# A hybrid two-layer model on one core: outer products of the palette stage taken over four parts of the array, and all engines' pieces in another order

## The reference, cut to what matters

```python
topk_val, topk_idx = jax.lax.top_k(logits, K)            # K = 15 nearest earlier tokens of every token
G = clip(einsum('bhtkd,bhtjd->bhtkj', P_sel_norm, P_sel_norm), -1, 1)
rel = concatenate([G, feat_a, delta]); h = gelu(rel @ W1 + b1); h = gelu(h @ W2 + b2)
z = tanh(h @ Wc + bc);  w = softmax(h @ Wm + bm)         # a point (gx, gy) and a weight for each neighbour
samples = bilinear samples of palette (128 x 16 x 16) at the 15 points
V = einsum('btkd,btk->btd', samples, w);  y = V @ Wo
```

## Time and profile before

| what | us |
|---|---|
| median of 3 runs | 1595.28 (1595.07 to 1597.09) |
| the profiled execution's own time | 1594.69 |
| its span, first to last instruction | 1592.5 |
| PE busy / DVE busy / ACT busy / POOL busy | 1301.1 / 1089.6 / 842.2 / 902.2 |
| mean granted TensorE clock, share of 2.4 GHz | 0.873 |

### The profile page before, as it was taken

The page is one execution under the profiler, slowest core; times in us unless marked ns, Lnnn a source line. Parts: engine busy times, 40 slices in busy tenths (PEclk is TensorE's granted clock), DMA queues, the critical chain, the costliest instruction groups (busy, mean ns, idle before and its releaser), DMA issues.

```text
span 1592.5 us, 47322 instructions
## 1 busy us (share of the span) xinstructions
PE 1301.1 (82%) x18392; PEld 861.7 (54%) x18501; DVE 1089.6 (68%) x4635; ACT 842.2 (53%) x2247; POOL 902.2 (57%) x1398
## 2 busy tenths in 40 slices
PE   3667678797889788887979798898978988788886
PEld 1333445454556555656556464656546565656654
DVE  2788677687778778787777777877866755464452
ACT  1233344464475555657564655475654646456665
POOL 2445666576658566666646565656645446455431
PEclk9686778897989889898989898898968888899999
DMA  5000000100000000000000000000000000000000
GB/s 159 2 1 10 27 18 18 29 9 23 6 25 9 25 7 17 17 11 24 17 22 8 18 14 14 20 7 24 9 18 14 7 27 10 26 15 21 5 3 7
DMA packets 27211, 29.57 MB, mean 19 GB/s; under 512 B 12097, under 2 KB 22114, under 8 KB 26978
## 3 DMA queue, kind: packets, MB, share of 16 engines
q0 software_dynamic: 8304, 16.73, 3.8%
q1 hardware_dynamic: 18674, 9.72, 2.2%
HBM read 25.11 MB, written 2.29 MB: 17 GB/s over the span
## 4 chain that ended last, share of the span: by engine, by line
PE 47%; DVE 22%; issue 10%; ACT 8%; POOL 8%; another core or an unknown queue 1%; SPq 1%; DMA 1%; DVEq 0%; POOLq 0%; ACTq 0%
DVE ps L963 4%; PE ps L665 3%; PE ps L523 3%; PE ps L717 3%; PE ps L747 3%; PE ps L563 3%; DVE ps L955 3%; PE ps L739 2%; PE ps L690 2%; PE ps L577 2%; PE ps L587 2%; PE ps L604 2%; PE ps L855 2%; ACT sb L1602 1%
## 5 line engine op out<-in xcount | busy, mean ns | idle before, releaser
L963 DVE TENSOR_TENSOR_SCAN ps<-ps,sb 128x47 f32<-128x47 f32 (+3 forms) x1024 | 271.3, 265 | 43.6 <-DVE ps L955 0.5
L1792 POOL DMA_INDIRECT sb<-table,sb x240 | 240.8, 1003 | 98.9 <-issue 55.3
L955 DVE TENSOR_TENSOR ps<-sb,ps 128x24 f32<-128x24 f32 (+3 forms) x1024 | 193.7, 189 | 15.4
L1656 POOL TENSOR_TENSOR sb<-sb 128x1 f32<-128x1 f32 x128 | 73.1, 571 | 221.4 <-DVE sb L898 220.7
L523 PE MATMUL ps<-sb 128*128 128x512 bf16 x496 | 162.0, 438 | 16.6 <-issue 10.2
L587 PEld LDWEIGHTS ps<-sb 32*32 32x32 f32 x2032 | 43.3, 110 | 123.9 <-issue 66.1
L577 PE MATMUL ps<-sb 32*32 32x32 f32 x2032 | 71.5, 213 | 41.5 <-DVE sb L935 34.6
L577 PEld LDWEIGHTS ps<-sb 32*32 32x32 f32 x2032 | 42.5, 111 | 113.2 <-DVE sb L935 58.5
L587 PE MATMUL ps<-sb 32*32 32x12 f32 x2032 | 65.5, 190 | 46.0 <-DVE sb L971 34.6
L1301 ACT ACTIVATE sb<-sb 128x128 f32<-128x128 f32 x128 | 62.9, 493 | 73.1 <-POOL sb L1658 72.8
L523 PEld LDWEIGHTS ps<-sb 128*128 128x128 bf16 x605 | 59.3, 109 | 62.5 <-issue 27.5
(11 more groups left out here) (310 smaller groups left out, 3739.4 us busy)
## 6 DMA issues: line engine op xcount, KB each, us to landing
sb<-table,sb POOLq DMA_INDIRECT x240
sb<-in_cs SPq DMA_DIRECT2D x16, 128.0 KB
table<-sb SPq DMA_DIRECT2D x17, 64.0 KB, 1.5
sb<-in_x SPq DMA_DIRECT2D x4, 256.0 KB, 7.8
sb<-dscr SPq DMA_DIRECT2D x64, 2.0 KB
out<-sb SPq DMA_DIRECT2D x16, 64.0 KB
sb<-in_mdn POOLq DMA_DIRECT2D x1, 512.0 KB, 9.9
sb<-in_wex SPq DMA_DIRECT2D x1, 512.0 KB, 7.4
```

Source lines behind the costliest of these rows:

```text
L955: e.tensor_tensor(at(psP, p + ROW - 3 - 2 * m, [ROW, 3], [2, m], [1, 2]), AC[:, row(n, k), :, HIST - 2 * m:HIST].rearrange("p r (a b) -> p ...
L963: e.tensor_tensor_scan(at(psD, 16 + k + COMB * skip, [COMB, 3 * ROW - skip]), at(psP, p + skip, [1, 3 * ROW - skip]), Q[:, i % 32, skip:3 ...
L1656: e.tensor_tensor(st[:, 11:12], st[:, 10:11], mhalf[:, 0:1], ALU.pow).then_inc(*s.G("lr"))
L1792: e.indirect_dma_start(GA[:, k, :], None, table[0:128 * i + 128, :] if i else table0, bass.IndirectOffsetOnAxis(u[:, k:k + 1], 0)).then_in ...
```

## The change

In stage mix on PE, the loop over the 32 outer products of a row group is made a loop over 16, with the two halves of it (u) inside: per k the order is now (row group 0, column part 0), (row group 1, column part 2), (row group 0, column part 1), (row group 1, column part 3). The number of matmuls, their shapes, operands and results, the bank, the 8 pieces of 8 matmuls and the waits are what they were.

```diff
-            for k in range(32):
-                if k % 4 == 0:
+            for k in range(16):
+                if k % 2 == 0:
                     yield
                     w.wait_ge(*m_.G.at("u4", c))
-                for g in range(2):
-                    rows, to = slice(64 * g, 64 * g + 64), 64 * g + 32 * (k // 16)
-                    x = e.matmul(pb[to:to + 32, 16 * (k % 16):16 * (k % 16) + 16], hats[rows, 512 + 32 * k:544 + 32 * k],
-                                 hats[rows, 16 * k:16 * k + 16], start=True, stop=True)
+                for u in range(2):
+                    for g in range(2):
+                        rows, to, n = slice(64 * g, 64 * g + 64), 64 * g + 32 * u, 16 * u + k
+                        x = e.matmul(pb[to:to + 32, 16 * k:16 * k + 16], hats[rows, 512 + 32 * n:544 + 32 * n],
+                                     hats[rows, 16 * n:16 * n + 16], start=True, stop=True)
             x.then_inc(*m_.P("op"))
```

```diff
 ORDER = {
     "PE":
-        "fffssggffgsssgsfssgssssgfssfssgsssssssssssfsgssssgosoossossfsosfgssoossssaasasssgasaassasasasgsspsspsssspfsps"
...
 FILL = (
-    "9190090520020000011000100000000000101010100000000000500000060000000320060020000000000030000000004010102000002000"
+    "9199012000040060040060200020020203010100000000000000600000400000000720090100002000200010000001002020002000000020"
...
```

More of the change, by code:

```diff
@@ new lines @@
+        "sosgsosposgsoosssssssoossssasapapssssafaasaasasfgsmspsmspsmsmsgommpsfspsoommsommspmmsomssgsmsmosmsosfsmmmmss"
+        "afsasasssasaassaasasmgmspsmsmgmmspmmpspmsmmsosmssoosoosfsmmsgmsmmsospomsmmpsasmgaamssmmmgmsmmsaaspmmasmmpasa"
+        "fasfsbbssbsmmmmmspmbbpbpsmbmsbbsmmsmmslolgsososososlsllsfsmllmgmsmlsmlsmlposposcmccccsmmmsmacsmgcacsmcpsamfs"
+        "ssmsdmdadspdmsmdmmaafgsdaaddadsssgssbmssbbosgmspfomopmmsbmpbboosbbbmmsmmmslsmlgmsmmoslslsosllllsmgpmsmpplsma"
+        "mlmmaasgcmcsccccmsmpsmccsmscfmssesmeeeeamsmmesedasseadsesdddagaamsmfmdddsmmdbmspbmmsobspmmsmmpsoooobbsbmbfsb"
@@ new lines @@
+        "sbmmmslopslospmsmpsgsmllllllmammsaamlmlspgsmsmmmfccmsacmsmcaspmccasscscfcaaaseeseedsemesmemesbdesdsdbmsmbpmm"
+        "msdgopmmmsdmdddbbobosbbsbososlglfsmsssloslollsllsmmmsplgslpaspamscacmsmmmmmcppcmsgcmcsmccmscsamasemeemsdmeam"
+        "seedfeddsaasdaefesdmmdsmmsmmmsddmbgbbmmsosmmpfspbsosobobsombsbsbgmsmsmsmlmsolsopsmmsppllspllpmallmsmamgfagsl"
+        "mmlmsmfmmcamsmcscccscsaascsasacsacgsmemseemmedemmmemsmmsmesmdsbdsdbedbosedsddpfdoobsosobpbgbsbbmsmmlmslsmmsm"
+        "mmmsposmlosmllslpppllamsagamsmmlmlmsgfmmscfcacccsscsaccssacasaapeeedemesmesessemsdesmmddsbbmmspdsmbpgodgdmdd"
@@ new lines @@
+        "mbmsomsobsbosobssbbmmmsmsmpmmslmlmsmmsomopslspllslslalpasafsllmsmcmccmgcmcmscmmgccscsaaaeseedmeemsempmsmamsa"
+        "aesedsemddsmbdsbbpdspdmmsddmmbogsfbsboosobsosbbmfsmmmlslsmmsmmpmospposmllsllallmsagsamssfpllgmmgsmmccccmsmmm"
+        "scacscaacscsaaseaeseseeesdmsemmpsedsemmsddbpsmmdmbbpsmmmddmosdfdbbboosobsobbfsmglsslsmsommosllslspllsmlpsmms"
+        "mmpmlsflpgcsacmcccscmmmcgcmscasmsaeesemesmmmesgdseesedadseddgassmmmmaddmsmmdpdamsafasmsmmmsobbsbsooosobpbbfp"
+        "bsbsbmmmsmolsmmslsommpsmsmfgsmmllslsllpslmgsmlmslmspasmcaccccsmmmscasscsscppscgsgememmmemdemmmeddmmmsmedemea"
@@ new lines @@
+        "dsaaesaasasogdsddsbdmsbbsoosoosbmsbpbpsbmbbmsmsmmmmpsommoplpslssmmsllllsallsammalmslmmsmpsccpcccccscceeeesdm"
+        "memsmmmemmeaedasesadddamsmmsaamddsddbsbbmmopmmoopbmobbobbbpsmmmmmmllmpmpmllllsolloppmlmalamamcccmmccccccaaed"
+        "eaedddemmmmdmmeaeaeaemdddebdmbbmmmpmpmbmbbmmbpbbmmmppbmpblblmmmmpmlmlllbllbmbmbblblmmmmlclcccclclllccllclele"
+        "ededeeddedemmmmemmmmmmmmcmmcmcddddbmbbcmmmcmcmmmmbcbbmcbbbcmmlmldemmmmddeeddllellellmmmmmmmmeeddeddlelmmmmcc"
+        "cbcbcbccccbbbebeeebbededleldeddlllllleldldddccccccccceededeedddeeeddeddeeeeeeeee",
@@ new lines @@
+    "DVE":
+        "fffffssssssssssssssssfssssfssssssssssssssssssssssssssssfsfssssssssssssssssssssssssssssssssssssssssssssssssss"
+        "sfsssssssfssssssssssssssssssssssssssssssssssssssssssssssssssssssssssssssssssssssssssssssssssfsfsssssssssssss"
+        "sssssssssssssssssssssssssssssssssssssfsssfsosassssssssssssssssssasssssssssasssssssssaasssassssssssaassssssss"
+        "ssssssssssssssasssspsssssssssssssssssssssssssssssssssssssssssssssssssssssssppsssssssspsffpsssspsssssssssssss"
+        "ssssssspsssssssssssssssssssssssssssssssssssssssssosssssasssssssssssssssssssasssssssassssssssaassassssssssaas"
+        "sssssssssssssasssspsssssfsssssssssssssssssfssssssssssssssssssssssssssssssssssspfssssfsssspssssmsssssssssssss"
+        "sssssssspsspsssssssssssspssssssssosssssssasssssmpssmssmssssssssssassssfsssssssssasssassaassssssssssasssassfs"
+        "ssssssssssssssssapsssssssssssssssssssssssssssssssssssssssssssmssssssssssssssssssssssssssssssssssfsssssssssfs"
+        "sssssssssosssssasssssspssspssssspsssspssspamssasssssaaspsssssassssssssssasassssssmsmssssssssasbsspfssssssssb"
+        "sssssssmsssssssbbbbsfssssbsbssssssssssssssssbslsssssssssmssssssssssssssssssssssssssssssssssssssssssssslslsff"
+        "lssslsssslslssssssssssslscssssssosssassscsssspsscpssssmssspssssasppsspcdsssssssssssssssssssasassssassassssss"
+        "sssssdsssssdddamassfsmssmsasbssdsssssssssssssssssspsfsssssssssssssssssbssssssssssbsbsbsbffsbbssssssblsssssss"
+        "ssssssssssmsssssssssssssssssssssssssssssssoslssssslasssllssssllpslcssssspsssssassspcsspsssmassssascssssspsss"
+        "saspssssscsesssssssssssssssdasessssssssmssssesmsssassssssassssssssssssmsedsddssdasssbpssssfssssdsssssssfssss"
+        "ssssssbssssbmssbssbssbsbbssssssssssssssbslsfssssssssssssssossfsssssassssssspspsppspsssllslslsllsssmssplssssa"
+        "ssssssacsssssassaacsssssssssamsamssssssssssssmsscsssssscsesdsssssassbsssesepsssssssssssssssfsssessssssssssss"
+        "sssdsfsdsssssddsbbsbbbsdmssbsbssssssssssssssbslsssssssssssssssssssssssssssssssssfsfsssssossssslssssslssalsll"
+        "lssssssslsscssssssssssssspssscpassmsscsspspasasssssassspasspcessssssasdssssssssessaemsssmsssssssssssdsdmdsss"
+        "adsesssssbsssfssssssssfssdpssbsssssssssssssbmbssbsssbssssssssssssssbsbsfssfssssssssssssbsslsssssssssssssssss"
+        "sssssssssssssssssoassspssppssssssspslslllssalslsamasaslssssssssscsapsssmssscsmssssscsssssasssaspssssssssssss"
+        "sssfssmssapcedssssssssfssssssssesbsssssssssssessssmsssssssssssdsdsddsbbessbbsbsssdssssssssssfsbsbsssfsssssss"
+        "blsssssssssssssssssssssssssssssssssssssossmaslsslssspspsspsplslsssaslslasssalcsssasspsssspamsssmcsssssssscss"
+        "asssssssssfsssscasdsssesmsssassspsesbsssesssssssssssssssssssssssssessssdssssssssssdbssdfdsbsbbbdsssssssssssm"
+        "sssssssssbbsssssssssssbssslssssssssssssssssssssssssssssossssssssssssssasssssssssmslsslasslslssslsslsssaslscs"
+        "passpcassffspsmpmssscasspcssessdssasspsssmsssassesssssessssssssssssssapbsssssssesssssdsssdsssdssbssdbssbsbsb"
+        "dssssmssssssbsbsssssssssssssssssssssbslsssssssssssssssssssssssssssfsssssssosssassssssfsslssslalsssssslsslsss"
+        "mslssssssasaslpcppssapsscsssssafsmssscssmsssspsapsssssssasscesfssdssssssssmassssesebssssssssssssssssssssssss"
+        "sspssesssssssddsssdbssdbssbssbmbssdsssbsbssssssssssblsssssssfssssssssssssssssssssssssssssssosfssssssssssssas"
+        "sslssssssslllsslsssllsscsspsfsfssssssscspssmpscsppssspscessssdssssssssssassasssssssesesmsssssssssssssmasasas"
+        "sssssessdsmddssssdassssasssssssssssssssdasbssssssssmssssssssspbsbsbsssssbbsssssssbbsssfssssssssssbslssssfsss"
+        "sssssssssssosssssssssssssassssssssssssssslsssmsssssssfllllslssssssslcssssssssssssssssscsssssmsssssssssmsssss"
+        "sascsmsssssasssssssassscsdsespspssepsespsaspsmdassdsspssdsasasesssdsssssasssbssssssssssssssdsssssssssspbssbs"
+        "sssssssbbbsssssssssbbsssssssssbssssslssssssssossmssssssassssssssssssssssssssssssllssssslllslssaslscssssssass"
+        "massssmsscapcppcessmdsspsesesssassssssspssasesssssassdpdsdsssdsssasbmssssssssdspsssssssbsssssssssbbbbbbblmll"
+        "oallllplcppacmcampaaamcedpaeapeddddapbedbbbbmbbbbblbbbmbpbpllbbllllplblmcmcpcplmlcedllllleedddecdmbcpdcbbbbb"
+        "mbbblcdemmeddmdedlllllldlecmbccbbbbbcedbbebleddddllllllelcdcccedeedddddeeeee",
@@ new lines @@
+    "ACT":
+        "ffffffffffffgfgfsffgfsfgffsfffgffffgsfffgfgfffsfgofoooofofogfsffsofaaaaaaasgpppgpppfpspfffffosgoopooosogoasa"
+        "apfpaaapaffgfpfmfpmpmmsgoppspffffppfooooopomfgmmofsmafmmafpaaffaafmmsappgsppmgpoooosofoffffommmmpgopppspaapg"
+        "aaasammgpfmmamffmpffbbfbmpmbbbfpbsppmllollgooooollfffmfflomsmmppgloppfpcfcccccccscacpcccpagcacmpmdsapfaammdd"
+        "ddadmgsffmfmmfbbgbbobgbffpfffsopobopoomollllgmommlllmpfppagplpaspapacgapcccfccccccacccmmsccpmfmeeeeeeeeaeede"
+        "emeesdmeddmddmffgfbpbfmbobbbppooobooosfmfffmfmlmsloppplplppgflalflaaalaamgmmcmfcccpsccaccmcccpmpccccmfmfefed"
+        "eeeeeeseeedeebeebddddfpbbpbmpogbboooolololsglfffmffolllmmmlpppagpapspcccaacacccacccccsgmcmccmfamefeeedeeedee"
+        "ememeddfeeddmmefffpbfbspmbgbobbppfpfffpfboosooomomgmmlplfpolslppppflaallagaafasglmmmmfppccfcfmccacccmccccccm"
```

(20 more changed lines are left out.)

124 lines of the change are left out of this document (21 added, 103 removed).

## The result

The changed kernel takes 1560.05 us (median of 4 runs, 1558.61 to 1561.05) against 1596.18 us of the kernel before beside it: ratio 0.9772, 95% interval 0.9755 to 0.9789. That is 36 us faster, where 7 were forecast, and outside the range. Times are medians; a ratio is worked out from the single runs and can differ from the ratio of the medians by a few tenths of a percent. A part of what follows rests on one fact that no single trace shows: chips differ. The kernel before takes 1596 us in the first comparison and 1600 us in one later set of runs (which chip the first one ran on is not recorded, so it may be the same), and 1486 to 1491 us on three other chips, and the ratio is not the same on them.

What follows compares the result with a forecast made beforehand. PE's pace and its waits were taken to bound the kernel; 5.4 us from the loop, 1.5 from the order and 0 from FILL made 6.9 us off 1594.69, 1587.8, stated as 1588.0 us, range 1576 to 1599.

Steps and rivals of the forecast that it cites:

- What bounds the kernel: Whole kernel: how tightly PE's pieces follow each other, plus waits for other engines; PE idles 291 of 1592.5 us.
- (a), the pace: Line 747's outer products over four parts: 16.7 ns a record falls to 11.6 (ends 8.3 and 15.2), saving 14.0 us.
- the 9 us of PE time before the factor of 0.6: Line 747's saving after losses to stops; 0.6 of it was to reach the end, 5.4 us.
- (a), the stops: Line 747 beside the gathers: 21% of records wait for issue anyway, so 14.0 us saved shrinks to 11.1.
- the 2 us for new stops: Line 747: denser runs may bring stops of their own, up to 4.7 us; 2 taken off the saving.
- (b), the order: All engines' pieces, moved mostly by a few places: only waits change, bound 16 us either way, 1.5 us gain taken.
- the third rival: The order brings more than the pace: two trains fewer or 20 us less recurrence waits, 1574 to 1582; chance 0.13.
- the second rival: Lines 747 and 739: new order brings two tiles more under the gathers, slower, 1598; chance 0.17.
- The price of a stop: Trains beside the gathers: two tiles more cost 13 us of PE time, 0.75 of it on the chain, +10.
- (c), FILL: Filling matmuls, line 523: 18 more in all, put where PE waits anyway, counted as 0.
- no faster pace: Line 747: four parts overlap less than read, 1591 if weights bind, 1594 to 1595 if one bank forbids it; chance 0.2.
- More stops: Same as the second rival: more tiles under the gathers, 1598, chance 0.17.

Runs made afterwards that it cites:

- e10: The kernel before, unchanged, profiled on a chip without stops: 1489.6 us.
- e16: Kernel before with the loop over four parts and each of 206 non-zero filling digits one higher (793 matmuls for 605), chip with stops: 1590.7 us, 0.9958.
- e17: Changed kernel with the old filling digits, each moved along with its piece, all 605 issued, chip with stops: 1573.6 us, 0.9877 of the kernel before.
- e3: Changed kernel with the old filling digits left at their old places, 85 of 605 matmuls falling away: 1521.1 us, 1.0206 of the kernel before.
- e9: Kernel before with the new order and filling digits but the old loop, second time, chip without stops: 1495.2 us, 1.0038.
- e2: Kernel before with the new order and filling digits but the old loop, first time, other chip: 1488.7 us, 0.9994.

## Why the prediction was wrong, by its own steps

- **What bounds the kernel.** Right: PE's pieces and its waits. The rows of the stops were read rightly as a cost of their own, 91.6 us, in trains beside the gathers. One comparison was wrong: the 9.3 us ahead of line 717 are PE's alone, the 48.8 and 42.8 are PE and weight loads. Counted like those, line 717 has 27.4 us before, and 24.4 in e10, where the other two lines have hardly any. So its idle time is for the most part something else than the trains.
- **(a), the pace.** The mechanism held: a part's own turn was the limit, and with four parts the pace fell to half, 8.4 to 8.9 ns, the lower end of the range (8.3), not the 11.6 of line 717 that was taken. At the low clock 14.0 came for 13.9. I took the row with the same 16 moving columns; the row that was nearer was the kernel's own switch at k = 16, which had shown both pairs of parts together. What was named as the next limit, handing over weights and columns at 11 to 15.2 ns, does not bind at 8.4. (The saving at the upper end, 8.1 us, should have been 7.6: at 15.2 ns the low clock's 13.9 can't be reached either.) Busy time of the line with the loop alone fell from 56.3 to 41.4 us, 14.9 against the 14.0 worked out. At the end 1600.2 x 0.0053 = 8.5 us came of it where 5.4 were forecast, and on the chips without stops 0.56% to 0.81%, 8 to 12 us. Both the 5.4 and the 9 us of PE time before the factor of 0.6 lie inside the interval, 2 to 15 us.
- **(a), the stops.** That the loop would not remove the trains was right. That a quicker array waits longer in them, and the 2 us for new stops, do not show: with the loop alone 91.6 us became 83.7, no more. Both were taken off the saving, and the saving came out larger (8.5 for 5.4), though within the noise of either.
- **(b), the order.** This is the step that failed: "I take 1.5 us for that, and zero for the rest". The order alone brought 1.8%, 29 us, on a chip with stops, where the text's own bound was 16 us. The mechanism was in the text, as the third rival (two trains fewer, 1574 to 1582), with 0.13 for it and too small a price. No ground was given for that chance; against the second rival, which turns on the same trains, it was said that mix and near move by 0.1 places on average. A mean over 512 pieces says nothing of one block against one train of gathers. At the twelfth tile the outer products came for the most part ahead of the gathers in place of under them, and took 4.5 us with the order alone and 6.5 with the loop alone, for 11.7 before. Over both lines PE's own stops fell by 24 us with the order alone, from 40.3 to 5.6 + 10.7 = 16.3.
- **The price of a stop.** I priced a train at 0.75 of its length. The same kernel on a chip with stops and on one without (first trace and e10) gives 73 - 12 = 61 us of idle for issue against 105 us of span, and PE is busy for at least 27 us longer, at a granted clock of 0.873 in place of 0.904. If the stops are all in which the chips differ, which isn't shown, one us of them costs 1.7 us, an estimate. For the order alone it would make 23 us of stops worth 40, where 29 to 31 were measured, so it is at the high end.
- **(c), FILL.** Counted at 0. That the number of digits is no cost was borne out: 188 more were none either (e16). What the new digits bring is open: with the old ones moved along the kernel took 1573.6 us (e17), about 1% over what the two parts' product gives, not beyond the noise. In e3 2.9% was lost when 85 of them fell away and the rest stood beside other pieces; which of the two it was isn't told apart.
- **The rivals.** Of "no faster pace" nothing is left: neighbours in the new order differ in rows and write to one bank, at 8.4 ns a record. By the rule of the Trainium skill (TensorEngine Tiling (Array Packing), Gotcha 1: PSUM Pressure) they could not. The measured 8.4 ns decides against it in this kernel, as it does against the floor of about 25 ns from start to start in the Trainium skill (TensorE: Matmul & The Clock Gate, "Wait — 56ns, not 53.3ns?"). "More stops" went the other way.
- **The sum.** On the chips without stops the pair comes out at 0.998 to 0.999: there the 36 us don't hold, and the pair gains less than the loop alone: the order gives back part of what the loop brings (e9: 1.0038, though e2 had 0.9994).

## What to carry to other kernels

Where a trace shows idle time that it calls issue, in trains at certain places, the order of pieces can decide how many of them are met: compare, block by block, what lies beside them, not how far pieces moved on average. A train can cost more than its length, as the engine's clock and the waits behind it change too. Before an order that was tuned by measurement is called better, time both on more than one chip: here the same pair of kernels gave 0.977 on one and 0.998 on another. The small matmuls here ran twice as fast over four parts of the array as over two, and a place where a kernel happens to use all four already shows that they overlap.

## What was not expected of the hardware

The same program took 1596 and 1600 us in two sets of runs, on one chip or two, and 1486 to 1491 us on three others. On the former, runs of small matmuls near indirect gathers break off every few records for half a microsecond; on the latter 80 such records pass beside a gather in 1.51 us, and idle for issue ahead of the two lines is 5.1 us in place of 91.6. The granted clock differs with it, 0.873 against 0.904. Matmuls of 64 rows by 32 columns with 16 moving columns, over four parts of the array, start every 8.4 to 8.9 ns at the higher clock and every 14.0 ns at the lower.
